# Layer 3's gather indices in four buffers, reloaded three chunks ahead, in place of two

## The reference

```python
def _L3_gnn_ref(x, edge_attr, W, root, gamma, beta, edge_index):
    ...
    src, dst = (edge_index[0], edge_index[1])
    weights, idx = _spline_basis(edge_attr)
    B = jnp.zeros((Etot, S), dtype=x.dtype).at[jnp.arange(Etot)[:, None], idx].add(weights)
    xj = x[src]
    z = (B[:, :, None] * xj[:, None, :]).reshape(Etot, S * x.shape[1])
    msg = z @ W.reshape(S * x.shape[1], W.shape[2])
    agg = jax.ops.segment_sum(msg, dst, num_segments=x.shape[0])
    ...
```

## Time and profile before

| | |
|---|---|
| median of 3 runs | 11,548.99 us |
| runs | 11,494.93 to 11,647.08 us |
| profiled execution, its span (no other time of it is recorded) | 11,537.7 us |
| POOL busy in the whole span | 6,567.8 us (57%), 6,626 instructions |
| DVE busy | 6,821.8 us (59%) |
| ACT busy | 4,714.2 us (41%) |
| PE busy | 3,146.5 us (27%) |
| layer 3's gathers, line 2445 | 1,568, 1,487.5 us busy |

### The profile page before, as it was taken

One profiled execution on the slowest core, in us unless ns is written; L12 is line 12 of the kernel. 1 busy time (PEld: TensorE's weight loads), 2 busy tenths in 40 slices (PEclk: granted clock), 3 DMA queues, 4 the chain that ended last, 5 costly groups with the idle time before them and its releaser, 6 DMA issues. The chain is left out here.

```text
span 11537.7 us, 92744 instructions
## 1 busy us (share of the span) xinstructions
PE 3146.5 (27%) x19432; PEld 2586.9 (22%) x19432; DVE 6821.8 (59%) x9436; ACT 4714.2 (41%) x6523; POOL 6567.8 (57%) x6626
## 2 busy tenths in 40 slices
PE   1111588882000000000023555555554200000002
PEld 1111477772000000000013444444443100000001
DVE  6777666664222311159962777777775566666664
ACT  1111466661211111137731666666662343334342
POOL 5656666665677777730023666666662466666663
PEclk9999767675555555555555677776775655555555
DMA  3332322222333323235522444444441666666662
GB/s 91 88 83 78 80 60 71 71 82 26 121 112 111 107 94 106 103 125 207 205 104 52 117 118 124 117 116 122 118 117 39 194 202 201 199 202 205 203 201 70
DMA packets 722783, 1395.92 MB, mean 121 GB/s; under 512 B 409552, under 2 KB 439453, under 8 KB 715095
## 3 DMA queue, kind: packets, MB, share of 16 engines
q0 software_dynamic: 287072, 587.19, 19.4%
q1 hardware_dynamic: 406786, 639.32, 17.0%
q10 hardware_dynamic: 28852, 168.65, 4.0%
HBM read 827.48 MB, written 602.51 MB: 124 GB/s over the span
## 5 line engine op out<-in xcount | busy, mean ns | idle before, releaser
L822 POOL DMA_INDIRECT l_rows<-in_x,l_idx x1568 | 1613.7, 1029 | 1010.1 <-issue 431.0
L2445 POOL DMA_INDIRECT l_rows<-table,l_idx x1568 | 1487.5, 949 | 1032.2 <-issue 483.2
L1925 POOL DMA_INDIRECT l_rows<-h,l_idx x1568 | 1540.3, 982 | 882.1 <-issue 442.4
L1303 POOL DMA_INDIRECT rows<-l_rows,l_idx x1568 | 1548.9, 988 | 554.0 <-issue 526.3
L1960 PE MATMUL l_made<-l_kv_w,l_rows_t 128*128 128x256 f32 x3136 | 1117.3, 514 | 1041.1 <-ACT l_kv L1990 402.5
L1960 PEld LDWEIGHTS l_made<-l_kv_w,l_rows_t 128*128 128x128 f32 x3136 | 761.2, 259 | 1279.5 <-issue 1147.1
L2521 ACT ACTIVATE l_lifted<-l_rows,l_up 128x256 f32<-128x256 f32 x1568 | 653.2, 463 | 824.0 <-DVE l_half_low L2473 527.1
L1698 PE MATMUL l_wide<-l_diag,l_ones 128*128 128x384 f32 x4 | 3.3, 926 | 3218.0 <-DVEq L1728 3218.0
L1259 ACT COPY l_rows<-l_run 128x1792 f32<-128x1792 f32 x56 | 191.6, 3421 | 1636.1 <-POOLq L88 1359.5
L1292 DVE TENSOR_TENSOR l_rows<-l_run,l_weights_ps 128x56 f32<-128x56 f32 x56 | 12.0, 215 | 1371.0 <-POOLq L88 1168.7
L1698 PEld LDWEIGHTS l_wide<-l_diag,l_ones 128*128 128x128 f32 x4 | 1.0, 312 | 3218.9 <-DVEq L1728 3218.9
(11 more groups left out here) (393 smaller groups left out, 12672.9 us busy)
## 6 DMA issues: line engine op xcount, KB each, us to landing
sums<-l1s_out ACTq DMA_DIRECT2D x56, 1988.0 KB, 7.1
sums<-l_out SPq DMA_DIRECT2D x112, 924.0 KB
spread<-zeros SPq DMA_DIRECT2D x28, 3612.0 KB
l_spread<-spread SPq DMA_DIRECT2D x112, 903.0 KB
l1s_rows<-rows SPq DMA_DIRECT2D x56, 1008.0 KB, 4.7
spread<-zeros SPq DMA_DIRECT2D x56, 938.0 KB
l_spread<-spread SPq DMA_DIRECT2D x56, 938.0 KB
sums<-l_out ACTq DMA_DIRECT2D x56, 896.0 KB
```

The costliest lines, as they stand in the source:

```text
L822: pool.indirect_dma_start(rows[:, b, t], None, a["x"], bass.IndirectOffsetOnAxis(ap=idx[:, b, t:t + 1], axis=0)) \
L1303: pool.indirect_dma_start(g["rows1_d"], bass.IndirectOffsetOnAxis(ap=idx[:, b, t:t + 1], axis=0), rows[:, b, t], None).then_inc(sent[b], 16)
L1925: pool.indirect_dma_start(rows[:, c.r, t, 0:C], None, g["h2_d"], bass.IndirectOffsetOnAxis(ap=idx[:, c.r, t:t + 1], axis=0)).then_inc(got[ ...
L2445: pool.indirect_dma_start(rows[:, b, t], None, g["table3_d"], bass.IndirectOffsetOnAxis(ap=idx[:, b, t:t + 1], axis=0)) \
```

## The change

`idx` gets four buffers and `idx_in` four semaphores, one each per place in a turn of four chunks. The first four chunks' indices are loaded at the start. The load that chunk c's landed rows release is that of chunk c+4, where it was that of chunk c+2; its place in SP's order, ahead of chunk c's store, is as before. Rows and output buffers stay double. SP's and POOL's loops now go over four chunks; as 98 is 24 x 4 + 2, SP runs 23 turns and then six chunks written out, and POOL 24 turns and then two chunks written out. DVE and ACT are as before.

```diff
--- before.py
+++ after.py
@@ -2386,7 +2386,7 @@
     K = T // GROUP
     with ExitStack() as stack:
         s = Space(nc, stack)
-        idx = s.sb("l3_idx", [P, 2, T], I32)
+        idx = s.sb("l3_idx", [P, UNROLL, T], I32)
         rows = s.sb("l3_rows", [P, 2, T, S3 * C])
         keep = s.sb("l3_keep", [P, 2, C, T])
         run = s.sb("l3_run", [P, 2, C, T])
@@ -2401,8 +2401,9 @@
         half_high = s.ps("l3_half_high", [P, GROUP, 2 * C])
         quarter = s.ps("l3_quarter", [P, GROUP, 2 * C])
         two = lambda n: [sem(f"l3_{n}{b}") for b in range(2)]
-        idx_in, keep_ready, scanned, copied, stored, lifted_ready, lifted_used, up_ready = (two(n) for n in (
-            "idx_in", "keep_ready", "scanned", "copied", "stored", "lifted_ready", "lifted_used", "up_ready"))
+        idx_in = [sem(f"l3_idx_in{r}") for r in range(UNROLL)]
+        keep_ready, scanned, copied, stored, lifted_ready, lifted_used, up_ready = (two(n) for n in (
+            "keep_ready", "scanned", "copied", "stored", "lifted_ready", "lifted_used", "up_ready"))
         got, rows_used = ([two(f"{n}{b}_") for b in range(2)] for n in ("got", "rows_used"))
         loaded, flags = sem("l3_loaded"), sem("l3_flags")
         with nc.Block() as block:
@@ -2410,41 +2411,50 @@
             def _(sp):
                 src = g["run_of"](g["e"]["src"], 1)
                 sums_v = g["run_of"](g["sums3_d"], C)
-                for b in range(2):
-                    sp.dma_start(idx[:, b], src[:, b * T:(b + 1) * T]).then_inc(idx_in[b], 16)
+                for r in range(UNROLL):
+                    sp.dma_start(idx[:, r], src[:, r * T:(r + 1) * T]).then_inc(idx_in[r], 16)
                 sp.dma_start(keys[:], g["run_of"](g["e"]["dst"], 1)).then_inc(loaded, 16)
                 sp.dma_start(prev[:], g["run_of"](g["e"]["dst_before"], 1)).then_inc(loaded, 16)
                 sp.dma_start(frac[:], g["run_of"](g["e"]["attr3"], D3)).then_inc(loaded, 16)
 
-                def indices(h, b):
-                    sp.dma_start(idx[:, b], src[:, bass.ds((h * 2 + b) * T, T)]).then_inc(idx_in[b], 16)
-
-                def store(h, b):
-                    wait(sp, copied[b], h + 2)
-                    sp.dma_start(sums_v[:, bass.ds((h * 2 + b) * (T * C), T * C)],
-                                 outb[:, b].rearrange("p t f -> p (t f)")).then_inc(stored[b], 16)
-
-                with sp.Fori(0, NC // 2 - 1) as h:
-                    for b in range(2):
-                        wait(sp, got[b][1], (h + 1) * (16 * HALF))
-                        indices(h + 1, b)
-                        store(h, b)
-                for b in range(2):
-                    store(NC // 2 - 1, b)
+                def indices(c):
+                    wait(sp, got[c.b][1], (c.h + 1) * (16 * HALF))
+                    sp.dma_start(idx[:, c.r], src[:, bass.ds((c.at + UNROLL) * T, T)]).then_inc(idx_in[c.r], 16)
+
+                def store(c):
+                    wait(sp, copied[c.b], c.h + 2)
+                    sp.dma_start(sums_v[:, bass.ds(c.at * (T * C), T * C)],
+                                 outb[:, c.b].rearrange("p t f -> p (t f)")).then_inc(stored[c.b], 16)
+
+                whole, rest = divmod(NC, UNROLL)
+                with sp.Fori(0, whole - 1) as n:
+                    for r in range(UNROLL):
+                        indices(Chunk(n, r))
+                        store(Chunk(n, r))
+                for r in range(UNROLL):
+                    if r < rest:
+                        indices(Chunk(whole - 1, r))
+                    store(Chunk(whole - 1, r))
+                for r in range(rest):
+                    store(Chunk(whole, r))
                 for b in range(2):
                     sp.wait_ge(stored[b], 16 * (NC // 2 + 1))
 
             @block.gpsimd
             def _(pool):
-                with pool.Fori(0, NC // 2) as h:
-                    for b in range(2):
-                        wait(pool, idx_in[b], (h + 1) * 16)
-                        for t in range(T):
-                            if t % HALF == 0:
-                                wait(pool, rows_used[b][t // HALF], h + 1)
-                            pool.indirect_dma_start(rows[:, b, t], None, g["table3_d"],
-                                                    bass.IndirectOffsetOnAxis(ap=idx[:, b, t:t + 1], axis=0)) \
-                                .then_inc(got[b][t // HALF], 16)
+                def gather(c):
+                    wait(pool, idx_in[c.r], (c.g + 1) * 16)
+                    for t in range(T):
+                        if t % HALF == 0:
+                            wait(pool, rows_used[c.b][t // HALF], c.h + 1)
+                        pool.indirect_dma_start(rows[:, c.b, t], None, g["table3_d"],
+                                                bass.IndirectOffsetOnAxis(ap=idx[:, c.r, t:t + 1], axis=0)) \
+                            .then_inc(got[c.b][t // HALF], 16)
+
+                for c in chunks(pool, NC // UNROLL * UNROLL):
+                    gather(c)
+                for r in range(NC % UNROLL):
+                    gather(Chunk(NC // UNROLL, r))
 
             @block.vector
             def _(v):
```

## The result

| | before | after |
|---|---|---|
| median of 20 runs | 11,557.15 us | 11,625.18 us |
| runs | 11,448.57 to 11,670.64 | 11,512.23 to 11,712.02 |
| ratio, 95% interval | | 1.0069 [1.0037, 1.0102] |
| span of the profiled execution | 11,537.7 | 11,618.4 |
| layer 3's gathers, first to last start | 2,289.3 | 2,332.3 |

The kernel is slower by 0.6 to 0.7%. The ratio leaves out each kernel's slower runs (over 1.5% above its fastest: 7 before, 3 after), while the medians in the table are of all 20 and lie 68 us apart. The median lies inside the forecast range and the loss is under 2%, but with 20 runs on each side it is clear of noise, and I had forecast no change.

A forecast was written before the change was run, and what follows sets the result against it. It took DVE's own stalls behind drains, not POOL, to bound layer 3's gather stage. All terms were 0: 11,537.7 + 0 = 11,537.7 us, stated as 11,546 towards the runs' median of 11,549; range 11,430 to 11,640.

The forecast's parts named there:

- What bounds the kernel: Layer 3's gathers: DVE's own stalls behind drains, some 6.5 us a chunk, set the pace; DVE never short of rows.
- Index waits go: POOL's gathers in layer 3: loads two chunks earlier remove all 30 index waits, offering POOL 94.5 us.
- What comes next: POOL next waits for DVE's free half: index waits' value taken as 0, drain waits growing from 216 to some 310 us.
- The slow rival: Longer POOL runs stall DVE more: 235 us to 11,784, chance 0.06; half of it, 11,666, chance 0.08.
- Loop bodies and start: POOL's loop of 64 gathers in place of 32, cost 0; four first loads, at most 0.8 us, taken as 0.
- The port rule: By the skill, line 2482 would not contend with GpSimd, so stalls would be unrelated to POOL; prediction went by the rows.

The follow-up runs named there:

- e1: Changed kernel with four index buffers and long loops, but each load fetches chunk c+2 again; ratio to the kernel before 1.0009, on a chip without stalls.
- e5: Kernel before, with SP's index load that chunk c+1 releases sent ahead of chunk c's store; ratio to the kernel before 1.0045, on a chip with stalls.
- e3: Changed kernel with POOL waiting at each chunk's end until its 16 gathers have landed; stage 2,403.4 us with stalls; without, 2,399.4 us, ratio to before 1.0442.
- g2: Changed kernel with POOL waiting after each chunk's eighth gather until all eight have landed; ratio to the kernel before 0.9965, on a chip with stalls.

## Why the prediction was wrong

*What bounds the kernel*: right for chips with stalls. DVE never waited for rows, before or after, and its own stalls made the pace. What I did not know is that this holds on some chips only; nothing in this one trace showed it.

*Index waits go*: right, all 30 of them (31 with the first).

*What comes next*: this is the step that failed. I took the value of an index wait on the path as 0, from two stretches of six chunks with 140.34 and 140.32 us, and let the drain waits grow from 216 to 310. They grew to 394. The value is below nothing: 56.8 us of loss for 30 waits, 1.9 us each. The two stretches compared one mixture of short pauses with another and said nothing of POOL with no index wait in the steady state, which takes 143.5 us for six chunks. The one with fewer index waits began behind a drain wait of 11.09 us, and had three more pauses of 1.65 to 1.86 us that I left out of the count (the other had one). I had written in this same step that pauses of any origin may let DVE recover, and had put it among the rivals.

*The slow rival*: its mechanism is what happened, at a quarter of its size. The pace is 23.9 us a chunk against the 25.8 that I took from the stage's first chunks, and DVE's stalls rose by 49 us in all, not by 235. The start, when POOL fills four empty halves and runs for 64 gathers, is worse than the steady cycle with its runs of 32. The code alone does not set that length: it hangs on how fast DVE frees the halves (the kernel before has runs of 48 too, and in e1, without stalls, POOL never stops). But the price of a run of 40 us stood in the trace, for such runs occurred before too: the one from 9,973.39 us ends in the wait before 10,016.89.

*The end of the stage*: not costed at all. POOL's greater lead at its last gather costs 13.9 us, a quarter of the loss.

*Loop bodies and start*: rightly taken as 0. e5 gets the same loss without them, and e1's long loops cost nothing that can be measured. The Trainium skill (Runtime: NRT & Kernel Launch, Instruction fetch mechanics) would have a taken branch outside the two resident pages cost a fetch; no run here shows it for a body of 64 gathers.

*The port rule*: by the Trainium skill (SBUF — State Buffer, Who interferes with whom) line 2482, with one SBUF input, does not contend with GpSimd. I had taken this to mean that the stalls would have nothing to do with POOL, and that is not so: e3 and g2 remove them by nothing but POOL's pauses. The rule itself is not shown wrong by it. Line 2482 takes its 0.42 us as ever, and the time is lost ahead of it; and SP, which does no SBUF arithmetic, is slowed on the same chips.

## What to carry to other kernels

A wait that ends early enough to be harmless may still be doing work: before removing one, ask what the engine does with the time, and look for a row in which the wait is truly absent and the steady state is reached, not one in which there are fewer of them. When two engines are coupled through buffers and one is slowed by the other's activity, the length of the faster one's bursts, which the buffers' depth and the slower one's pace set together, is the quantity to price. And price what is left at the end of a stage whenever a producer gets a larger lead.

## What the runs showed of the hardware

The same kernel took 10,390 us on three chips and 11,670 to 11,855 on three others, more than any edit tried here. Layer 3's stage is only a part of it: some 1,960 us in e1 against 2,304 in the kernel before on chip 2. The code ahead of the stage is the same in all these kernels, and the stage's first gather starts at 8,228 to 8,281 us on the one kind and at 9,037 to 9,355 on the other; what makes that difference was not looked at.

On the latter kind DVE stalls behind its drains when POOL has issued indirect gathers for long enough without a pause. In the steady cycle of the changed kernel that is 20.6 us into a run. It is no fixed length: in the first run of the stage the stalls begin after 38 us in its first profile, and in the kernel before a run that follows on a run of 40 us and a pause of 3.7 us has them from its start. Per chunk of 20 us a pause of 0.6 us does not help, 1.9 us takes away a seventh of the stalls, 3.2 us all of them; 8.5 us behind every 40 us does not keep them away. Halving the bytes changes nothing.

SP is slowed too, but not at the same moments. Its register instruction ahead of an index load, in the kernel before and in e3, both on chip 2 (ns, min/median/max):

```profile
...
L2420 SPq FUSED_REGOPS  x96: 3/700/737, 9378.6 to 11634.7; - x96
...
```

```profile
...
L2422 SPq FUSED_REGOPS  x92: 46/46/60, 9363.0 to 11600.7; - x92
...
```

This reads as if POOL's pause had cured SP as well. Its issue of the store, in e3 again and then in e1 on a chip without stalls, says that it had not:

```profile
...
L2426 SPq DMA_DIRECT2D sums<-l_out x98: 7/701/738, 9382.3 to 11761.4; - x98
...
```

```profile
...
L2427 SPq DMA_DIRECT2D sums<-l_out x98: 337/350/361, 8268.9 to 10208.4; - x98
...
```

0.701 us in the median against 0.350, though DVE has no stalls in e3. In e3 the index load goes out while POOL stands still, the store some 18 us into its next run. And e5, which has all of DVE's stalls, has 0.053 us in the median for the register instruction. So SP's time tells what POOL did just before, and not whether DVE stalls. What the sequencers wait for, and why only on some chips, is not settled by these runs.
